# Attention score units: plain and diagonal ones merged three to two

## The chip, the cores and the metric

The program runs on one core of one Trainium2 chip. The metric is the device time of the whole program in microseconds, the median of several runs. Engines: TensorE (PE, its weight loads PEld), VectorE (DVE), ScalarE (ACT), GpSimd (POOL) and SyncE (SP), which issues the DMAs.

## What is computed

A transformer layer over 2048 tokens of width 512: layer norm, causal attention with 16 heads of 32, and beside it a feed-forward part with 4-bit weights. The change touches the attention alone. Cut to that:

```python
xn = _layernorm(x, axis=-1)
qkv = einsum('bsh,oh->bso', xn, w_qkv)            # 16 heads, head_dim 32
scores = einsum('bhqd,bhkd->bhqk', q, k) / sqrt(32)
scores = where(causal, scores, finfo.min)
probs = softmax(scores, axis=-1)
attn = einsum('bhqk,bhkd->bhqd', probs, v)
x = x + einsum('bsh,oh->bso', attn, w_o) + ffn(xn)
```

## The kernel before, in words

Three stages follow each other: layer norm and projection, attention (function `attention`), output projection and feed-forward. Attention takes the heads in eight pairs (`PAIRS`); `a` is the head of a pair, 0 or 1.

For each pair the scores are computed twice. The first time they stand plainly, queries on the partitions, only to find each query's largest score. A **unit** (`UNITS`, line 344; function `scores`, line 848, matmul at L855) is one such matmul: query tile `i` of 128 queries (16 of them) against up to 512 keys, key block `b`. For `b` under `i // 4` the unit lies left of the diagonal and is 512 columns wide. For `b == i // 4` it lies on the diagonal and is 128, 256, 384 or 512 wide (`P * (i % 4 + 1)`). A pair has 80 units: 48 left of the diagonal, 32 on it. They go round four banks (`p_s`). VectorE reduces each to its maximum (`unit_max`, line 759): L771 for the left ones, L767 with the mask for the diagonal ones. When the last unit of a query chunk `r` (four query tiles, `UNITS_TO[r]`) is reduced, VectorE joins the parts (`join_parts`, L778), GpSimd splits the maxima into three bf16 parts (`split`, five small instructions, L650 to L658), TensorE turns them (`turn_max`, L865, four small matmuls), and ScalarE copies them into rows of `q_stack` (`max_row`, L691), where the second computation of the scores subtracts them.

The second time the scores stand transposed, keys on the partitions. A pair has 40 steps (`STEPS`): chunk `qc` of 512 queries against key tile `kt`; each step has a **score tile** for each head (`scores_t`, L883; on the diagonal also `mask_t`, L892). The tiles go round three banks. ScalarE takes the exponential into `e_sb` (`exps`, L708), TensorE multiplies by the values (`product_v`, L909), GpSimd, at the end also VectorE, sums pairs of `e_sb` (`sum_steps`, L635 and L816) and TensorE sums those over the partitions (`row_sums`, L923). At a chunk's end ScalarE copies the output (`copy_out`, L720); GpSimd later multiplies it by the reciprocal sums (`normalise`, L668).

The order is written out. The loop `for k in range(NG)` (line 964) makes 80 **passes** of four steps each, ten to a pair; in this text pass 0 to 9 is `k` modulo 10. Pass `k` issues on TensorE: the eight score tiles of the *next* pass's steps, the first seven eighths of the pass's units in between, turned maxima if any are due, the row sums of the pass before, the products of this pass's steps, in passes 0, 2, 5, 9 (which multiply diagonal steps) also their row sums, and then the last eighth of the units. Score tiles on the diagonal (narrower, masked) are issued in passes 1, 4, 8 and 9: the **diagonal passes** of this text; the others are **plain passes**. In a plain pass two units follow the third tile, one the fourth, one the fifth, two the sixth, one the seventh. In a diagonal pass three follow the first two tiles, one the next two, two the next two, one the last two.

The units run ahead of the steps (`UNITS_AHEAD`, 56). The first pass takes 12 units, passes 1 to 72 take eight each, the last seven none. Units 1 to 44 stand earlier still, four or five behind each value tile of the stage's start. GpSimd's program in pass `k`: the second half of this pass's sums, the first half of the next's, the splits whose units end in this pass (`BATCHES[k]`), a `normalise` in passes 3, 4, 6, 7. The turns' passes (`TURNS`) don't depend on the units' order: chunk 0 in pass 8, chunk 1 in pass 9, chunk 2 in pass 1, chunk 3 in pass 4.

## Time and profile before

| | |
|---|---|
| median of 3 runs | 1840.53 us (1839.3 to 1840.86) |
| profiled execution | 1840.19 us, span 1838.4 us |
| TensorE busy | 1796.9 us, 98% |
| VectorE busy | 1127.0 us, 61% |
| ScalarE busy | 702.3 us, 38% |
| GpSimd busy | 721.6 us, 39% |
| plain score units L855 | 640 matmuls, 217.2 us busy |
| maxima L771 and L767 | 384 and 256 units, 241.2 and 119.7 us busy |
| sums on GpSimd L635 | 244, 291.2 us busy |

The span is the time from the first to the last instruction of the profiled execution; the run's time is 1.8 us longer. The first unit starts at 137 us, the passes run from 180 to 726 us, and the feed-forward part ends the span. Busy times are unions of recorded intervals. A matmul's record includes its way through the array, so TensorE counts as busy while it issues less than it could: what counts is the distance between starts.

### The profile page before, as it was taken

The numbers are of one execution on the slowest core, as the hardware profiler recorded it, in microseconds if no ns is written. First come the engines' busy times: TensorE is split into PE (matmuls) and PEld (weight loads), VectorE is DVE, ScalarE is ACT, GpSimd is POOL, SyncE is SP. The second block draws the span as 40 slices with busy tenths as digits, with TensorE's granted clock in tenths as the row PEclk, the third lists the DMA queues.
The fourth block names the chain that finished last, engine by engine and source line by source line (L and its number), as shares of the span: only waits on it lengthen the run. The fifth ranks groups of instructions, "written<-read, shape, count | busy, mean of one in ns | idle before, by whom it ended". The sixth has DMA issues, their size and how long they took to land.

```text
span 1838.4 us, 28874 instructions
## 1 busy us (share of the span) xinstructions
PE 1796.9 (98%) x10496; PEld 1348.4 (73%) x10496; DVE 1127.0 (61%) x1724; ACT 702.3 (38%) x1151; POOL 721.6 (39%) x720
## 2 busy tenths in 40 slices
PE   7989999999999998999999999999999999999998
PEld 6877666666666654478888888888888888888887
DVE  5416666666666666457665675666566567566654
ACT  3323666666666664023232332232232323323322
POOL 1431778778778774021222222222222222222221
PEclk9999999999999998999999999999999999999999
DMA  8675043143143100521101101100110110110002
GB/s 286 218 215 151 10 102 73 37 102 73 37 102 72 38 17 21 197 69 35 35 0 34 34 0 34 34 26 9 34 34 0 34 34 3 31 34 0 1 1 92
DMA packets 73105, 108.59 MB, mean 59 GB/s; under 512 B 24704, under 2 KB 44784, under 8 KB 69360
## 3 DMA queue, kind: packets, MB, share of 16 engines
q1 hardware_dynamic: 73008, 107.34, 21.2%
q8 instruction: 56, 0.92, 0.2%
q14 instruction: 41, 0.34, 0.1%
HBM read 74.04 MB, written 29.59 MB: 56 GB/s over the span
## 4 chain that ended last, share of the span: by engine, by line
PE 60%; DVE 0%; issue 0%
PE p_up L51 6%; PE p_gate L51 6%; PE p_gate L49 6%; PE p_up L49 6%; PE p_gate L50 6%; PE p_up L50 6%; PE p_out L51 6%; PE p_out L49 6%; PE p_out L50 6%; PE p_out L1358 1%; PE p_gate L1358 1%; PE p_up L1358 1%; DVE acc L1288 0%
## 5 line engine op out<-in xcount | busy, mean ns | idle before, releaser
L1200 POOL TENSOR_SCALAR poly<-poly 128x1024 f32<-128x1024 f32 (+1 forms) x65 | 71.4, 1098 | 841.3 <-ACT poly L1162 841.3
L635 POOL TENSOR_TENSOR e_sum<-e_sb 128x512 f32<-128x512 f32 (+1 forms) x244 | 291.2, 1220 | 99.2 <-PE p_o L923 89.8
L771 DVE TENSOR_REDUCE max_part<-p_s 128x1 f32<-128x512 f32 x384 | 241.2, 683 | 51.5 <-PE p_s L855 50.2
L708 ACT ACTIVATE e_sb<-p_v 128x512 f32<-128x512 f32 (+3 forms) x427 | 216.5, 552 | 129.7 <-PE p_v L883 70.2
L1263 DVE SCALAR_TENSOR_TENSOR inter<-inter,gate 128x1024 f32<-128x1024 f32 (+1 forms) x65 | 78.6, 1209 | 248.4 <-ACT inter L1168 247.6
L855 PE MATMUL p_s<-k_stack,q_stack 96*128 96x512 f32 (+3 forms) x640 | 217.2, 393 | 0.7 <-DVE max_part L771 0.5
L767 DVE CUSTOM_DVE_ANT_0 recip<-p_s,score_mask 128x128 bf16<-128x128 f32 (+3 forms) x256 | 119.7, 486 | 156.0 <-PE p_s L855 153.9
L1161 ACT ACTIVATE gate<-p_gate 128x1024 f32<-128x1024 f32 (+1 forms) x65 | 66.0, 1015 | 354.6 <-PE p_gate L51 354.6
L49 PE MATMUL p_gate<-xn_hi,w_hi 128*128 128x512 f32 x512 | 199.6, 390 | 0.0
L50 PE MATMUL p_gate<-xn_lo,w_hi 128*128 128x512 f32 x512 | 199.2, 389 | 0.0
L51 PE MATMUL p_gate<-xn_hi,w_lo 128*128 128x512 f32 x512 | 199.2, 389 | 0.0
L49 PE MATMUL p_up<-xn_hi,w_hi 128*128 128x512 f32 x512 | 199.2, 389 | 0.0
L50 PE MATMUL p_up<-xn_lo,w_hi 128*128 128x512 f32 x512 | 199.2, 389 | 0.0
L51 PE MATMUL p_up<-xn_hi,w_lo 128*128 128x512 f32 x512 | 199.2, 389 | 0.0
L49 PE MATMUL p_out<-i_hi,w_hi 128*128 128x512 f32 x504 | 196.1, 389 | 0.0
L50 PE MATMUL p_out<-i_lo,w_hi 128*128 128x512 f32 x504 | 196.1, 389 | 0.0
L51 PE MATMUL p_out<-i_hi,w_lo 128*128 128x512 f32 x504 | 196.1, 389 | 0.0
L1203 POOL TENSOR_TENSOR poly<-poly,gate 128x1024 f32<-128x1024 f32 (+1 forms) x65 | 177.8, 2735 | 5.4
L883 PE MATMUL p_v<-q_stack,k_stack 128*128 128x512 f32 (+3 forms) x427 | 159.2, 397 | 8.1 <-ACT e_sb L708 5.1
L855 PEld LDWEIGHTS p_s<-k_stack,q_stack 96*128 96x128 f32 x640 | 115.3, 189 | 47.0 <-issue 28.5
L909 PE MATMUL p_o<-e_sb,v_stack 128*32 128x256 f32 (+1 forms) x2304 | 148.6, 372 | 0.0
L1283 DVE TENSOR_TENSOR acc<-acc,p_out 128x2048 f32<-128x2048 f32 x63 | 143.6, 2280 | 3.3 <-PE p_out L51 3.3
(146 smaller groups left out, 3090.6 us busy)
## 6 DMA issues: line engine op xcount, KB each, us to landing
q_stack<-qk_scratch SPq DMA_DIRECT2D x48, 256.0 KB, 6.5
k_stack<-qk_scratch SPq DMA_DIRECT2D x48, 256.0 KB, 7.2
qk_scratch<-out_hi SPq DMA_DIRECT2D x32, 256.0 KB, 2.6
qk_scratch<-out_lo SPq DMA_DIRECT2D x32, 256.0 KB, 3.3
scales<-in_gate_up_s SPq DMA_DIRECT2D x128, 64.0 KB, 2.3
xn_lo_scratch<-xn_lo SPq DMA_DIRECT2D x4, 1024.0 KB, 5.2
v_scratch<-o_sb SPq DMA_DIRECT2D x16, 256.0 KB, 2.6
xn_lo<-xn_lo_scratch SPq DMA_DIRECT2D x1, 4096.0 KB, 16.7
```

The source lines that it names most:

```text
L49: nc.tensor.matmul(out, w_hi, x_hi, start=first, stop=False)
L50: nc.tensor.matmul(out, w_hi, x_lo, start=False, stop=False)
L51: return nc.tensor.matmul(out, w_lo, x_hi, start=False, stop=last)
L635: nc.gpsimd.tensor_tensor(*operands(k, i), ALU.add).then_inc(pool_summed, 1)
L708: nc.scalar.activation(e_sb[:, x % E_BUFS, 0:w], bank_st(x)[:, 0:w], ACT.Exp, scale=SCALE).then_inc(exp_done, 1)
L767: nc.vector.tensor_tensor_reduce(out=masked_scores[:, m % 2, 0:w], in0=p_s[:, slot[n] % S_BUFS, 0:w], in1=score_mask[:, W - w:], scale=1.0 ...
L771: nc.vector.reduce_max(part, p_s[:, slot[n] % S_BUFS, 0:w], AX.X).then_inc(maxed, 1)
L855: nc.tensor.matmul(p_s[:, slot[n] % S_BUFS, 0:w], q_stack[p % PB][a][0:ROWS, i * P:(i + 1) * P], k_stack[p % PB][a][0:ROWS, b * W:b * W + ...
L883: last = nc.tensor.matmul(bank_st(x)[:, 0:W - q0], k_stack[p % PB][a][:, kt * P:(kt + 1) * P], q_stack[p % PB][a][:, qc * W + q0:(qc + 1) ...
L909: last = nc.tensor.matmul(p_o[(2 * a + h) * D:(2 * a + h + 1) * D, 0, first - h * HALF:], v_stack[p % PB][:, kt, a, :], e_sb[:, (g * PIECE ...
L1203: nc.gpsimd.tensor_tensor(part_of(poly, h, parts), part_of(poly, h, parts), part_of(gate, h, parts), ALU.mult).then_inc(poly_done, 1)
L1283: nc.vector.tensor_tensor(here, here, p_out[:, :, :], ALU.add).then_inc(added, 1)
```

## The change

The list of units is put in another order. Before, it goes query tile by query tile: the left units of a tile, then its diagonal unit, for both heads. Now there are two lists, the left ones (`LEFT`) and the diagonal ones (`EDGE`), each in the order of query tiles, and five at a time are taken: one diagonal, two left, one diagonal, one left. Every unit keeps its operands and its width. `UNITS_TO` (after how many units a chunk's maxima are complete) was 8, 24, 48, 80 and is 19, 39, 59, 80. Head 1's first unit is the third instead of the second, hence `FIRST_OF`, where TensorE waits for the loaded heads.

```diff
-    UNITS = [(a, i, b, min(W, P * (i + 1) - b * W))
-             for r in range(TC) for i in range(4 * r, 4 * r + 4) for b in range(r + 1) for a in range(2)]
+
+    LEFT = [(a, i, b, W) for i in range(4, TT) for b in range(i // 4) for a in range(2)]
+    EDGE = [(a, i, i // 4, P * (i % 4 + 1)) for i in range(TT) for a in range(2)]
+    UNITS = [unit for n in range(TT) for unit in (EDGE[2 * n], LEFT[3 * n], LEFT[3 * n + 1], EDGE[2 * n + 1], LEFT[3 * n + 2])]
     NU = len(UNITS)
-    UNITS_TO = [sum(1 for a, i, b, w in UNITS if i < 4 * r + 4) for r in range(TC)]
+    UNITS_TO = [1 + max(u for u, (a, i, b, w) in enumerate(UNITS) if i < 4 * r + 4) for r in range(TC)]
     NUNIT = PAIRS * NU
+    FIRST_OF = [next(u for u, unit in enumerate(UNITS) if unit[0] == a) for a in range(2)]
...
-                if u < 2:
+                if u in FIRST_OF:
                     pe.wait_ge(qk_loaded[p % PB][a], 96 * (p // PB + 1))
```

The widths of a pass's eight units, worked out from the two lists (diagonal passes in bold):

| pass | before | now |
|---|---|---|
| 0 | 512 512 512 512 512 512 256 256 | 512 512 512 512 128 512 512 128 |
| **1** | 512 512 512 512 512 512 384 384 | 512 256 512 512 256 512 384 512 |
| 2 | 512 512 512 512 512 512 512 512 | 512 384 512 512 512 512 512 512 |
| 3 | 128 128 256 256 384 384 512 512 | 128 512 512 128 512 256 512 512 |
| **4** | 512 512 128 128 512 512 256 256 | 256 512 384 512 512 384 512 512 |
| 5 | 512 512 384 384 512 512 512 512 | 512 512 512 512 128 512 512 128 |
| 6 | 512 512 512 512 128 128 512 512 | 512 256 512 512 256 512 384 512 |
| 7 | 512 512 256 256 512 512 512 512 | 512 384 512 512 512 512 512 512 |
| **8** | 384 384 512 512 512 512 512 512 | 128 512 512 128 512 256 512 512 |
| **9** | 512 512 512 512 512 512 128 128 | 256 512 384 512 512 384 512 512 |

TensorE, pass 9 before, from the last score tiles to the first of the next pass (`p_s` are units, `p_v` and `p_st3` score tiles and their masks, `max_cols` the turned maxima, `p_o` row sums and products):

```order
L883 MATMUL p_v<-q_stack01,k_stack01 128x128
L892 MATMUL p_st3<-mask_k,ident_bf 128x128
L892 MATMUL p_v<-mask_k,ident_bf 128x128
L855 MATMUL p_s<-k_stack00,q_stack00 128x128
L865 MATMUL p_s<-ident_bf,max_cols 64x128 x4
L923 MATMUL p_o<-e_sum,ones 32x256 x8
...
L923 MATMUL p_o<-e_sum,ones 32x256 x2
L855 MATMUL p_s<-k_stack01,q_stack01 128x128
L883 MATMUL p_v<-q_stack00,k_stack00 128x512
```

The same place now:

```order
L886 MATMUL p_v<-q_stack01,k_stack01 128x128
L895 MATMUL p_st3<-mask_k,ident_bf 128x128
L895 MATMUL p_v<-mask_k,ident_bf 128x128
L858 MATMUL p_s<-k_stack00,q_stack00 128x512
L868 MATMUL p_s<-ident_bf,max_cols 64x128 x4
L926 MATMUL p_o<-e_sum,ones 32x256 x8
...
L926 MATMUL p_o<-e_sum,ones 32x256 x2
L858 MATMUL p_s<-k_stack00,q_stack00 128x512
L886 MATMUL p_v<-q_stack00,k_stack00 128x512
```

Units 7 and 8 of the pass were 128 wide and are 512 wide; nothing else moved.

TensorE, pass 1 before, from the first masks to the third and fourth score tile:

```order
L892 MATMUL p_v<-mask_k,ident_bf 128x128 x2
L855 MATMUL p_s<-k_stack00,q_stack00 128x512
L855 MATMUL p_s<-k_stack01,q_stack01 128x512
L855 MATMUL p_s<-k_stack00,q_stack00 128x512
L883 MATMUL p_st3<-q_stack00,k_stack00 128x384
```

The same place now:

```order
L895 MATMUL p_v<-mask_k,ident_bf 128x128 x2
L858 MATMUL p_s<-k_stack00,q_stack00 128x512
L858 MATMUL p_s<-k_stack00,q_stack00 128x256
L858 MATMUL p_s<-k_stack01,q_stack01 128x512
L886 MATMUL p_st3<-q_stack00,k_stack00 128x384
```

The second of the three units has 256 columns instead of 512.

GpSimd before, from the sums of pass 8 to those of pass 0 of the next pair (`max_cols` from `row_max` begins a split, `e_sum` are sums):

```order
L635 TENSOR_TENSOR e_sum<-e_sb_49 128x384 x2
L650 CAST max_cols<-row_max 128x2x4
L652 TENSOR_TENSOR rest1<-row_max,max_cols 128x2x4
L654 CAST max_cols<-rest1 128x2x4
L656 TENSOR_TENSOR rest2<-rest1,max_cols 128x2x4
L658 CAST max_cols<-rest2 128x2x4
L635 TENSOR_TENSOR e_sum<-e_sum,e_sb_49 128x256 x2
L635 TENSOR_TENSOR e_sum<-e_sum,e_sb_49 128x128 x2
L635 TENSOR_TENSOR e_sum<-e_sb_49 128x384 x2
L635 TENSOR_TENSOR e_sum<-e_sum,e_sb_49 128x256 x2
```

The same place now:

```order
L638 TENSOR_TENSOR e_sum<-e_sb_49 128x384 x2
L638 TENSOR_TENSOR e_sum<-e_sum,e_sb_49 128x256 x2
L638 TENSOR_TENSOR e_sum<-e_sum,e_sb_49 128x128 x2
L638 TENSOR_TENSOR e_sum<-e_sb_49 128x384 x2
L638 TENSOR_TENSOR e_sum<-e_sum,e_sb_49 128x256 x2
L638 TENSOR_TENSOR e_sum<-e_sum,e_sb_49 128x128 x2
L638 TENSOR_TENSOR e_sum<-e_sb_49 128x512 x2
L653 CAST max_cols<-row_max 128x2x4
L655 TENSOR_TENSOR rest1<-row_max,max_cols 128x2x4
```

The split of chunk 2 stood at the end of pass 8, ahead of the diagonal sums of pass 9. It now stands two passes later, at the end of pass 0, behind the diagonal sums of passes 9 and 0 and the first sums of pass 1.

## Rows read from the trace of the kernel before

**Rows 1.** One pair's length in windows: stretch, length, busy us per engine, granted clock, DMA.

```profile
199.00:268.00 69.00, 67.98 (x660) 42.93 (x658) 45.00 (x117) 42.97 (x92) 51.26 (x70) 1.00 0.31 66
```

**Rows 2.** ScalarE's timeline, pass 2: start, length, operation; the exponentials.

```profile
471.00 1.12 ACT L708 ACTIVATE e_sb<-p_v 128x512 f32<-128x512 f32 x2
471.95 0.66 ACT L708 ACTIVATE e_sb<-p_st 128x512 f32<-128x512 f32 x1
```

**Rows 3.** VectorE's timeline, pass 2 and the start of pass 3: maxima and a join.

```profile
469.77 3.68 DVE L771 TENSOR_REDUCE max_part<-p_s 128x1 f32<-128x512 f32 x6
...
476.60 0.19 DVE L778 TENSOR_REDUCE row_max<-max_part 128x8 f32<-128x32 f32 x1
```

**Rows 4.** Waits from 250 to 690 us: who for whom, us, times, longest.

```profile
PEld p_s L855 <- DVE max_part L771: 1.7, 7, 0.2
```

**Rows 5.** The same wait over the whole span.

```profile
PEld p_s L855 <- DVE max_part L771: 5.1, 15, 0.6
```

**Rows 6.** TensorE's weight loads, timeline in pass 5 of two pairs; idle before in brackets.

```profile
426.84 0.14 PEld L923 LDWEIGHTS p_o<-e_sb,ones 128*32 128x32 f32 x3 [0.77 <-POOL e_sum L635]
...
495.82 0.14 PEld L923 LDWEIGHTS p_o<-e_sb,ones 128*32 128x32 f32 x3 [0.77 <-POOL e_sum L635]
```

**Rows 7.** GpSimd's timeline, passes 4, 8 and 9; idle before in brackets.

```profile
487.42 4.46 POOL L635 TENSOR_TENSOR e_sum<-e_sb 128x512 f32<-128x512 f32 x4 [1.58 <-PE p_o L923]
...
515.35 4.46 POOL L635 TENSOR_TENSOR e_sum<-e_sb 128x512 f32<-128x512 f32 x4 [1.00 <-PE p_o L923]
519.74 0.23 POOL L650 CAST max_cols<-row_max 128x8 bf16<-128x8 f32 x1
...
521.03 2.25 POOL L635 TENSOR_TENSOR e_sum<-e_sum,e_sb 128x256 f32<-128x256 f32 x4
```

**Rows 8.** TensorE's timeline: unit 8 and the next tile (passes 9, 2), unit 7 (pass 0).

```profile
455.39 0.33 PE L855 MATMUL p_s<-k_stack,q_stack 96*128 96x128 f32 x1
455.55 0.45 PE L883 MATMUL p_v<-q_stack,k_stack 128*128 128x512 f32 x1
...
458.98 0.28 PE L855 MATMUL p_s<-k_stack,q_stack 96*128 96x256 f32 x1
459.13 0.50 PE L883 MATMUL p_st<-q_stack,k_stack 128*128 128x512 f32 x1
...
475.32 0.50 PE L855 MATMUL p_s<-k_stack,q_stack 96*128 96x512 f32 x1
475.66 0.40 PE L883 MATMUL p_v<-q_stack,k_stack 128*128 128x512 f32 x1
```

**Rows 9.** TensorE's timeline in diagonal passes: units 1 to 3 (pass 1), unit 7 (8, 9).

```profile
462.44 0.94 PE L855 MATMUL p_s<-k_stack,q_stack 96*128 96x512 f32 x3
463.22 0.34 PE L883 MATMUL p_st<-q_stack,k_stack 128*128 128x384 f32 x1
...
513.33 0.47 PE L855 MATMUL p_s<-k_stack,q_stack 96*128 96x512 f32 x1
513.74 0.35 PE L865 MATMUL p_s<-ident_bf,max_cols 128*64 128x128 bf16 x3
...
520.85 0.30 PE L855 MATMUL p_s<-k_stack,q_stack 96*128 96x128 f32 x1
521.08 0.41 PE L865 MATMUL p_s<-ident_bf,max_cols 128*64 128x128 bf16 x4
```

**Rows 10.** The first pass: VectorE's maxima, and TensorE's load for unit 10.

```profile
181.88 0.28 DVE L767 CUSTOM_DVE_ANT_0 recip<-p_s,score_mask 128x128 bf16<-128x128 f32 x1
...
182.29 3.67 DVE L771 TENSOR_REDUCE max_part<-p_s 128x1 f32<-128x512 f32 x6
...
183.63 0.19 PEld L855 LDWEIGHTS p_s<-k_stack,q_stack 96*128 96x128 f32 x1 [0.30 <-DVE max_part L771]
```

**Rows 11.** The longest pieces of the chain: start, us, what; the first matmuls behind attention.

```profile
731.16 9.96 PE p_gate L1358 x16
741.12 6.87 PE p_up L1358 x16
```

## The prediction, made before the kernel ran

> **What bounds the kernel now.** I read the page first, then attention in windows of one head pair, then one pair row by row, then the waits. TensorE was busy for 67.98 of the 69 us of a pair [rows 1], but that hides the real limit. Ten passes make one head pair, and they repeat: the same wait comes back at 426.84 and 495.82 [rows 6], 68.98 us apart. A pass has two halves. In the first, eight score tiles (L883) go round three banks: TensorE may write a tile only when ScalarE's exponential (L708) of the tile three back is done. The exponentials of wide tiles follow each other every 0.48 us (two from 471.00 on, the next at 471.95 [rows 2]), TensorE could deliver a wide matmul every 0.23 us (458.98 to 459.13 is 0.15 us with 256 columns; 475.32 to 475.66 is 0.34 us because a weight load isn't hidden [rows 8]). So in much of this half TensorE keeps step with ScalarE, and the plain score units (L855), which the change reorders, fill its gaps. In the second half TensorE alone sets the pace: row sums, products, and the eighth unit.
>
> Two engines that the change touches may give or take cover. VectorE takes the maxima, six wide ones in 3.68 us, 0.61 us each [rows 3]; it must stay within four banks of TensorE. It is busy 45.0 us in 69 [rows 1], and in 440 us of steady state TensorE's weight loads waited for it 1.7 us in all, never over 0.2 us [rows 4]. GpSimd is the fuller one, 51.3 us of 69 [rows 1], and TensorE waited for it once a pair, in pass 5: 0.77 us before the row sums at 495.82 [rows 6].
>
> **The change, part by part.** It removes and adds no matmul and no maximum. It moves three things.
>
> (a) *Widths inside a pass.* Units are numbered 1 to 8 as in the table above. What a narrow unit saves depends on who sets the pace where it stands.
>
> Unit 8 stands alone behind the products, on the path: to the start of the next score tile 0.34 us pass when it is 512 wide and 0.16 us when it is 128 (455.39 to 455.55) [rows 8]. A narrow one hides less of the weight load behind it, so I take 0.12 of these 0.18 us for a swap from 128 to 512, 0.07 from 384 to 512, nothing from 256 to 128. It gets wider in passes 1 (+0.07), 4 (+0.12) and 9 (+0.12), narrower in pass 5 (-0.12).
>
> Units 1 to 7 of a plain pass are paced by ScalarE where it is behind, as in passes 0, 3 and 6, in which it also copies the output. In pass 0 unit 7 grows from 256 to 512 columns: 0.15 us [rows 8] become 0.23, +0.08. In pass 6 it shrinks from 512 to 384, -0.07 at most by its columns, taken whole. In pass 7 units 3 and 4 grow from 256 to 512: 0.08 each, of which I take 0.14 in all. If this cover is complete both are 0.
>
> Units 1 to 3 of a diagonal pass (1, 4, 8, 9) stand between two pairs of tiles. In pass 1 three wide units take 0.78 us (462.44 to 463.22 [rows 9]) and TensorE sets the pace; pass 9 looks alike. They lose 256 and 384 columns, 0.12 and 0.17 us at 0.23 us for 512, but the second tile of the pair then waits for its exponential: -0.10 and -0.14. In passes 4 and 8 they hold 1152 before and after, and 1280 before and 1152 after: 0 and, as I read ScalarE's lead there, 0.
>
> Unit 7 of a diagonal pass stands before the turned maxima (L865) on the path: 0.23 us with 128 columns (520.85 to 521.08) against 0.41 us with 512 (513.33 to 513.74) [rows 9]. Pass 9 goes from the one to the other, +0.18; pass 4 from 256 to 512, between them, +0.12.
>
> By pass: 0: +0.08; 1: -0.03; 2, 3, 8: 0; 4: +0.24; 5: -0.12; 6: -0.07; 7: +0.14; 9: +0.16. Pass 4's unit 8 comes after the row sums on which GpSimd's chain for pass 5 starts, so its +0.12 only shortens the wait of 0.77 us. Sum: **+0.28 us a pair**. The ends, by columns: if all that units 7 and 8 gain is paid, 768 + 256 columns are +0.46 us; if all that units 1 to 3 of the diagonal passes lose counts and nothing added does, 768 columns are -0.35 us.
>
> (b) *VectorE's load.* Pass 2, with eight wide units, was its fullest (from 469.77 without a break [rows 3]); of the small waits in [rows 4] some 0.2 us a pair are its, and a 384-wide second unit takes them away: -0.07 a pair at the path, between 0 and -0.2. The joins of query chunks 0 to 2 now stand inside a pass: VectorE takes 0.19 us for one (476.60 [rows 3]), in engine time that it has.
>
> (c) *GpSimd's splits.* A split (L650 to L658) may run once its chunk's last unit is reduced. The chunks now end at units 19, 39, 59, 80 instead of 8, 24, 48, 80, so the splits of chunks 0, 1 and 2 move from passes 3, 5 and 8 to passes 5, 7 and 0 of the next pair. Each keeps GpSimd 1.3 us (519.74 to 521.03 [rows 7]). Leaving pass 3 gives nothing: GpSimd waited 1.58 us for TensorE behind it, at 487.42. In pass 5 one split replaces another, behind the sums that TensorE waits for. In pass 7 it eats the 1.00 us of idleness before 515.35 and delays the next sums by some 0.3 us; TensorE wants them a pass later, so 0. In pass 8 it goes away from ahead of pass 9's diagonal sums, which TensorE did not wait for: 0. In pass 0 it stands ahead of the turn of chunk 2 in pass 1, behind unit 7. Its unit is reduced some 8 us before that turn, and GpSimd has no more than its sums of the pass in between: 0, and without that cover up to its 1.3 us a pair.
>
> (d) *The start.* The first pass takes twelve units at once, and there VectorE sets the pace: unit 10 started at 183.63 when the maximum of unit 6 was done [rows 10]. Of the first six, two had 128 columns (0.41 us for both, 181.88 to 182.29). Now one of these is wide and the other 384: 0.61 + some 0.48, so +0.6 us once. Ahead of it, each burst of units behind a value tile now begins with a wide one, for whose maximum the fifth unit waits; it was narrow in five bursts. TensorE's loads waited 5.1 us for maxima in the whole trace [rows 5], 1.7 of them in steady state. Half a wait more for the five would be 1.4 us, none is 0; most of it hides behind matmuls under way, +0.2 us.
>
> **The sum.** Steady state +0.28 - 0.07 = +0.21 us a pair; 72 passes carry eight units, 7.2 pairs: +1.5 us. Start +0.8 us. Against the profiled execution's 1840.19 us (span 1838.4) that is 1842.5; that execution stands 0.3 us under the median, 1840.53, so the forecast of the median is **1842.8**. That is +0.12%, under the 0.2% (3.7 us) that a measurement of this kernel can tell from no change.
>
> A page speaks otherwise of VectorE. The row first: six wide maxima start and end within 3.68 us, so the next starts while the last still writes [rows 3]. The Trainium skill (VectorE: DVE Perf Modes, section The DRAIN you can't avoid) says that after each operation the pipe is emptied for about its duration less 266 ns before the next starts. By that, as an estimate from the page, a wide maximum would cost 0.6 us by duration and 0.35 us more, VectorE would be the bound of every pass, and since its total doesn't change, nor would a pair: the sum would be the start alone. The row contradicts it, and the sum goes by the row.
>
> **The rivals.**
> *Smoothing works (faster).* VectorE's and GpSimd's stalls shrink. For it: VectorE has 5.1 us of them [rows 5], GpSimd 0.77 us a pair [rows 6]. Against it: most of the first lie in the start, and GpSimd's chain from 487.42 to the sums at 495.82 (four sums, a product, four more) holds no split, so nothing leaves it. If all went: 1840.5 - 5.1 - 7 x 0.77 = 1830.0; half of it 1835. It decides where unit 5 to 7 of a wide pass now start earlier: 0.07.
> *Gains in the diagonal passes only.* -0.35 - 0.07 a pair and no losses: 1840.5 - 3.0 + 0.8 = 1838.3, within 0.2%: 0.12.
> *Wide units on the path (slower).* Units 7 and 8 are paid in full, 0.46 us, units 3 and 4 of passes 3, 5 and 7 lose their cover for another 0.3 us a pair, and the start costs its upper end, 2.0 us: 0.76 x 7.2 + 2.0 = +7.5, 1848.0. It decides where unit 7 is issued later than ScalarE frees its tile. For it: eight of ten seventh units are wide now, six before. Against it: ScalarE's copy of the output in passes 3 and 6. 0.22.
> *The split becomes the bound (slower).* (c) without cover, 1.3 us a pair: 1850. GpSimd would have to be several us later in pass 0: 0.03.
> *The clock at the hand-over.* TensorE's first 16 matmuls of the output projection took 9.96 us, the next 16 took 6.87 [rows 11]: it started at 1.2 GHz of its two levels. A shift of attention's end may add or take such a stretch, -3 to +3 us on top of any case, half the time nothing; it is in the range.
> That the order isn't what the change says has no chance left: TensorE's program shows the merge.
>
> **How the numbers follow.** The forecast case (1840 to 1844.2) has 0.56, the faster rival 0.07, the diagonal one 0.12, the slower ones 0.25. By sign, with some of the clock's swing: faster by over 0.2% (under 1836.9) 0.12, within 0.2% 0.62, slower (over 1844.2) 0.26. The range leaves out the far ends, 1835 and less and 1850, and reaches the slower rival's time: 1837.0 to 1848.0.
>
> **What would show it.** Right: pairs of 69.1 to 69.3 us; pass 5's wait for GpSimd still at 0.6 to 0.8 us; passes 4 and 9 longer by 0.1 to 0.25 us, pass 7 by 0.1; splits in passes 5, 7 and 0; unit 10 of the first pass 0.6 us later. Wrong: a pair under 68.7 us, pass 5's wait gone, or a wait of TensorE for GpSimd or for turned maxima that did not exist.

## The result, and the profile of the changed kernel

The changed kernel took 1846.16 us (median of 7 runs, 1843.42 to 1848.78) against 1840.76 us for the kernel before on the same chip: a ratio of 1.0027, 95% interval 1.0015 to 1.0039. Beside the last experiments it was measured again: 1844.79 us (11 runs) against 1840.66, 1.0024 with an interval of 1.0015 to 1.0033. By the medians it is 5.4 and 4.1 us slower, a little over the 0.2% that the forecast (+2.3 us, 1842.8) gave as the border, though both intervals begin below it. The profiled execution took 1843.77 us, its span 1842.0 us, 3.6 us more than before.

Where the 3.6 us are, from the starts of score tiles in both traces (L886 now, L883 before):

| place | before | now | longer by |
|---|---|---|---|
| first pass starts at | 179.21 | 180.47 | 1.26 |
| first pass | 7.52 | 8.24 | 0.72 |
| the other nine of the first ten | 61.93 | 62.45 | 0.52 |
| pairs 1 to 6, together | 413.78 | 414.91 | 1.13 |
| output projection starts at | 731.16 | 734.69 | 3.53 in all |

(The last pair's stretch is 0.1 us shorter now.) The start thus costs 1.98 us, the steady state 0.19 us a pair. The stretch behind attention is the same: the chain of the changed kernel (start, us, what), to be held against [rows 11]:

```profile
734.69 9.98 PE p_gate L1361 x16
744.67 6.87 PE p_up L1361 x16
```

One pair in windows (as [rows 1], the first window near the same place, the second from one pass 0 to the next). From one pass 0 to the next (455.55 to 524.53), TensorE was busy for 67.45 us before, VectorE for 45.01 and GpSimd for 55.63. TensorE's time has grown by 0.5 us, the others' have hardly moved, and no engine has become full:

```profile
200.00:269.00 69.00, 68.11 (x654) 42.16 (x650) 45.43 (x119) 42.98 (x92) 50.63 (x68) 1.00 0.29 63
458.65:527.75 69.10, 67.94 (x641) 41.98 (x640) 45.09 (x117) 42.98 (x92) 55.72 (x73) 1.00 0.33 71
```

TensorE's waits of the changed kernel from 250 to 690 us (who for whom, us in all, times, longest). VectorE's share is what it was [rows 4]; GpSimd's six waits, one a pair, fell from 0.77 to 0.55 us each:

```profile
PEld p_o L926 <- POOL e_sum L638: 3.3, 6, 0.6
...
PEld p_s L858 <- DVE max_part L770: 1.9, 6, 0.3
```

The wait itself, in pass 5, where [rows 6] had 0.77 us:

```profile
498.86 0.14 PEld L926 LDWEIGHTS p_o<-e_sb,ones 128*32 128x32 f32 x3 [0.54 <-POOL e_sum L638]
```

The ten passes of a pair, in us from one first score tile to the next, in each kernel that is told of below. The row of a kernel is that of its common pair: pairs 1 to 6 of one trace agree within 0.05 us in every pass, but for single long passes that are told of where they belong. Of *narrow at 3 or 5* it is the mean of its two variants:

| kernel | 0 | 1 | 2 | 3 | 4 | 5 | 6 | 7 | 8 | 9 | pair |
|---|---|---|---|---|---|---|---|---|---|---|---|
| before | 6.32 | 6.76 | 7.02 | 6.17 | 7.26 | 7.65 | 6.17 | 6.73 | 7.49 | 7.39 | 68.97 |
| changed | 6.22 | 6.84 | 6.95 | 6.16 | 7.49 | 7.36 | 6.22 | 6.73 | 7.48 | 7.71 | 69.15 |
| forecast, difference | +.08 | -.03 | -.07 | 0 | +.24 | -.24 | -.07 | +.14 | 0 | +.16 | +.21 |
| measured, difference | -.10 | +.08 | -.07 | -.01 | +.23 | -.29 | +.05 | 0 | -.01 | +.32 | +.19 |
| narrow last | 6.26 | 6.82 | 6.91 | 6.00 | 7.28 | 8.72 | 6.05 | 6.56 | 7.28 | 7.62 | 69.49 |
| wide last | 6.39 | 6.83 | 7.02 | 6.17 | 7.49 | 7.53 | 6.17 | 6.72 | 7.49 | 7.71 | 69.53 |
| split in pass 4 | 6.32 | 6.76 | 7.03 | 6.17 | 7.26 | 8.85 | 6.17 | 6.73 | 7.49 | 7.39 | 70.16 |
| narrow at 3 or 5 | 6.26 | 6.86 | 7.02 | 6.17 | 7.26 | 7.65 | 6.16 | 6.71 | 7.50 | 7.72 | 69.31 |
| placed | 6.20 | 6.66 | 6.82 | 6.04 | 7.31 | 7.48 | 6.04 | 6.49 | 7.27 | 7.42 | 67.73 |

(The forecast's pass 5 holds both its own -0.12 and the -0.12 by which pass 4's longer end was to shorten the wait.)

### The profile page after: what moved, and what is told of

It reads as the page before. It is cut to its first block, busy times and chain, and to the rows that moved or that the text cites. A ratio compares the mean times of both kernels' runs of the same rounds, so it can differ in the third digit from the quotient of the medians.

```text
span 1842.0 us, 28874 instructions
## 1 busy us (share of the span) xinstructions
PE 1801.9 (98%) x10496; PEld 1347.0 (73%) x10496; DVE 1128.0 (61%) x1724; ACT 702.7 (38%) x1151; POOL 723.3 (39%) x720
## 4 chain that ended last, share of the span: by engine, by line
PE 60%; DVE 0%; issue 0%
PE p_gate L51 6%; PE p_up L51 6%; PE p_gate L50 6%; PE p_gate L49 6%; PE p_up L50 6%; PE p_up L49 6%; PE p_out L51 6%; PE p_out L50 6%; PE p_out L49 6%; PE p_out L1361 1%; PE p_gate L1361 1%; PE p_up L1361 1%; DVE acc L1291 0%
## 5 line engine op out<-in xcount | busy, mean ns | idle before, releaser
L774 DVE TENSOR_REDUCE max_part<-p_s 128x1 f32<-128x512 f32 x384 | 256.7, 687 | 124.4 <-PE p_s L858 123.8
L770 DVE CUSTOM_DVE_ANT_0 recip<-p_s,score_mask 128x128 bf16<-128x128 f32 (+3 forms) x256 | 123.7, 483 | 85.8 <-PE p_s L858 83.7
L886 PE MATMUL p_v<-q_stack,k_stack 128*128 128x512 f32 (+3 forms) x427 | 160.2, 398 | 7.6 <-ACT e_sb L711 3.9
```

The lines of the kernel that those rows point to most:

```text
L770: nc.vector.tensor_tensor_reduce(out=masked_scores[:, m % 2, 0:w], in0=p_s[:, slot[n] % S_BUFS, 0:w], in1=score_mask[:, W - w:], scale=1.0 ...
L774: nc.vector.reduce_max(part, p_s[:, slot[n] % S_BUFS, 0:w], AX.X).then_inc(maxed, 1)
L886: last = nc.tensor.matmul(bank_st(x)[:, 0:W - q0], k_stack[p % PB][a][:, kt * P:(kt + 1) * P], q_stack[p % PB][a][:, qc * W + q0:(qc + 1) ...
```

## The experiments

All experiments but *the changed kernel again* hold one list of 80 units for each pair, `LISTS`: `OLD` is the order of before, `NEW` that of the change. What follows from a list (`UNITS_TO`, the splits' passes) is worked out from it as before.

### Which part of the time is the start's

The first kernel gives the first pair, whose units are those of the start, its old order and the others the new one, the second the other way round.

```diff
+    LISTS = [OLD] + [NEW] * (PAIRS - 1)
...
+    LISTS = [NEW] + [OLD] * (PAIRS - 1)
```

> The new order for head pairs 1 to 7, the old one for pair 0, so the start of attention is as it was before. Theory 'two parts' (the start costs 2.0 us once, each later pair 0.19 us): the first exponential starts at 176.2 us as before and not at 177.4, pairs take 69.16 us each, pass 9 is still 0.3 us longer, and the time is 1.3 to 1.7 us over the kernel before (ratio 1.0008). Theory 'steady state alone' (the start's delay is swallowed later): all of the 3.5 to 5 us stay, ratio 1.002 to 1.003.

> The other half: the new order for pair 0 alone, the old one for pairs 1 to 7. Theory 'two parts': first exponential at 177.4 us, unit 10 of the first pass some 0.7 us later still, pairs 1 to 6 at 68.97 us, time 2.0 to 2.3 us over before (ratio 1.0012). Theory 'steady state alone': within 0.5 us of before.

Medians: 1841.11 us for the first (ratio 1.0005, 0.9996 to 1.0014) and 1841.33 for the second (1.0009, 1.0000 to 1.0018): two halves that the time of the whole program can hardly tell from nothing. The traces can. Pairs take 69.15 us in the first and 68.94 in the second, the first pass 7.51 and 8.23. The stretch from the first unit to the first exponential, which holds the value tiles and their bursts, took 39.04 and 40.44 us, as in the kernels whose first pair they share (39.10 before, 40.46 changed). Its length has to be measured from its own first unit, since that starts anywhere from 137.0 to 140.7 us, whatever the kernel. In the seven traces here with the old first pair it took 38.99 to 39.10 us in five, and 39.31 and 39.40 in the two (*split in pass 4*, *narrow at 3 or 5*) in which TensorE's granted clock was still at 1.2 GHz when the first unit started; the three traces with the whole new first pair have 40.44 to 40.46. So the two costs belong to the two parts of the list and add up: +1.36 us ahead of the first pass, +0.72 in it, +0.19 a pair.

### The bursts behind the value tiles

```diff
+    def narrow_first():
+        out = list(NEW[:4])
+        for u in list(range(4, 44, 5)):
+            burst = NEW[u:u + 5]
+            out += sorted(burst, key=lambda unit: unit[3])
+        return out + NEW[44:]
+    LISTS = [narrow_first()] + [NEW] * (PAIRS - 1)
```

> The changed kernel, but in pair 0 each burst of units behind a value tile is sorted so that its narrowest unit comes first. Theory 'the fifth unit of a burst waits for the first one's maximum': the value stage takes 0.2 to 0.35 us less per burst, so the first exponential starts at 175.5 to 176.3 us instead of 177.4, and the time is 1.2 to 2 us under the changed kernel (ratio to before 1.0010 to 1.0016). Theory 'the sum of VectorE's work in the stage counts': first exponential stays at 177.4 us.

The median is 1842.78 us (1.0013, 1.0004 to 1.0023). The stretch took 38.62 us, 1.84 less than in the changed kernel and 0.48 less than before, with the same units in the same bursts. First pass and pairs are the changed kernel's (8.25, 69.15). TensorE's units in the changed kernel, in which every burst of five begins with a 512-wide unit and its last unit waits for the maximum of the first (in brackets the idle time and whom it waited for):

```profile
140.43 0.99 PE L858 MATMUL p_s<-k_stack,q_stack 96*128 96x512 f32 x4
...
141.61 0.39 PE L858 MATMUL p_s<-k_stack,q_stack 96*128 96x256 f32 x1 [0.19 <-DVE max_part L774]
...
144.58 1.62 PE L858 MATMUL p_s<-k_stack,q_stack 96*128 96x512 f32 x5
...
148.78 1.68 PE L858 MATMUL p_s<-k_stack,q_stack 96*128 96x512 f32 x5
```

The maximum that the fifth unit waited for, on VectorE:

```profile
140.87 0.69 DVE L774 TENSOR_REDUCE max_part<-p_s 128x1 f32<-128x512 f32 x1 [1.80 <-PE p_s L858]
```

Before, the third burst began narrow and was over sooner:

```profile
148.62 1.25 PE L855 MATMUL p_s<-k_stack,q_stack 96*128 96x256 f32 x5
...
152.46 1.50 PE L855 MATMUL p_s<-k_stack,q_stack 96*128 96x384 f32 x5
```

From burst to burst it is 4.15 to 4.26 us now, in all seven distances, and was 3.83 to 3.89 behind the three bursts that began with 128 or 256 columns before (148.62 to 152.46 is one). The brackets show 0.2 us of each wait. The rest hides in the pipelined records: the first four matmuls read 0.99 us, yet the fifth starts 1.18 us behind the first. In all traces it starts 1.18 us behind a first of 512 columns, 1.00 behind one of 384 and 0.81 or 0.82 behind one of 256.

Not all of the 1.36 us is this wait: 0.25 us lie between the first unit and the fifth of the stage (3.46 us now, 3.21 before), whose first four units hold 1280 columns instead of 768. The remaining 1.11 us are the bursts of five.

### Wide or narrow at the end of a pass

The first kernel sorts each pass's eight units by width, the second puts 128 columns at unit 8 and 256 at unit 7 wherever it has them; the first pair is the old one in both.

```diff
+    def wide_last():
+        out = []
+        for u in range(0, len(OLD), 8):
+            out += sorted(OLD[u:u + 8], key=lambda unit: unit[3])
+        return out
...
+    def narrow_last():
...
+            out.append(eighth.pop(0) if u % 8 == 7 else seventh.pop(0) if u % 8 == 6 and seventh else rest.pop(0))
```

> Pairs 1 to 7: the eight units of each pass of the old order, sorted so that the widest come last; no unit leaves its pass, chunk ends and splits stay. Pair 0 as before. Theory 'units 7 (diagonal passes) and 8 are on the path, others covered': pass 0 +0.1 us (unit 8 from 256 to 512), pass 1 +0.13, pass 4 +0.24 with pass 5 shorter by 0.1, pass 9 +0.3, the rest within 0.05, pairs at 69.5 to 69.7 us, ratio 1.0020 to 1.0030. Theory 'the mix of a pass decides' (VectorE's load per pass is unchanged): pairs at 68.97 us.

> Pair 0 as before; in pairs 1 to 7 the units are placed so that unit 8 of every pass is 128 wide (256 in passes 1 and 2) and unit 7 mostly 256. Theory 'place decides' (a narrow unit behind the products saves 0.12 us against a wide one, a narrow seventh 0.08 to 0.2 us in the passes where TensorE sets the pace there, elsewhere width is free): pass 2 to 8 each 0.1 to 0.2 us shorter, pairs at 67.9 to 68.4 us, time 4 to 7 us under before (ratio 0.997). Theory 'only the load on VectorE counts' (passes now hold up to seven wide units in a row): no gain, pairs at 68.9 to 69.5 us.

*Wide last* came to 1845.74 us (1.0022, 1.0013 to 1.0031), its pairs to 69.53 us, +0.56. It touches no chunk's order, so its splits stay, and the passes that got longer are those in which units 7 and 8 grew: 4 and 9 to exactly the changed kernel's 7.49 and 7.71. In pass 9 it gives units 1 and 2 only 128 columns, 768 fewer in all, and gets nothing for them: its pass 9 is as long as the changed kernel's.

*Narrow last* came to 1843.66 us (1.0020, 1.0011 to 1.0030), where 4 to 7 us less than before had been expected. Nine passes of its common pair sum to 60.77 us, against 61.32 before; pass 5 took 8.72 instead of 7.65 and ate twice that. The waits from 250 to 690 us name the place:

```profile
PEld p_o L941 <- POOL e_sum L653: 11.8, 6, 2.0
```

2.0 us a pair where there were 0.77. Its chunk 0 ended at unit 16, and so that split fell into pass 4, between the sums of pass 4 and those that pass 5's row sums wait for.

### The split, by itself

```diff
+    def swapped(u, v):
+        out = list(OLD)
...
+        out[u], out[v] = out[v], out[u]
+        return out
+    LISTS = [OLD] + [swapped(7, 8)] * (PAIRS - 1)
...
+    LISTS = [OLD] + [swapped(47, 56)] * (PAIRS - 1)
```

Both swap two units of 512 columns, so no width moves. In the first kernel, chunk 0 ends one unit later and its split goes from pass 3 to pass 4; in the second, chunk 2 ends nine units later and its split goes from pass 8 to pass 0.

> The old order with two units of the same width (512) exchanged in pairs 1 to 7, units 8 and 9 of the pair: chunk 0 ends one unit later, so its split moves from pass 3 to pass 4; widths, and all else, stay. Theory 'a split in pass 4 lies on the chain from the row sums of pass 3 to the diagonal sums of pass 5': pass 5 grows from 7.65 to 8.7 to 8.95 us, TensorE's wait for GpSimd in it from 0.77 to about 2.1 us, pairs at 70.0 to 70.3 us, 7 to 9 us in all, ratio 1.0040 to 1.0050. Rival 'GpSimd's order is free, it idles 1.6 us in pass 4': pairs at 68.97 us.

> The old order with two units of the same width (512) exchanged in pairs 1 to 7, so that chunk 2 ends at unit 57 instead of 48 and its split moves from pass 8 to pass 0 of the next pair, as in the changed kernel; widths stay. Theory 'covered': every pass within 0.02 us of before, pairs at 68.97 us, ratio 1.000. Rival 'the move out of pass 8 or into pass 0 is worth something': pass 9 shorter, or pass 0 or 1 longer, by 0.1 us or more.

The first came to 1850.22 us (1.0043, 1.0029 to 1.0056), the second to 1840.19 (0.9997, 0.9988 to 1.0006). One unit's place costs 1.2 us a pair, another's nothing. Pass 5 took 8.85 us (7.65 before), all other passes their old times. GpSimd of the first, from pass 4 on (start, us, line, operation, in brackets idle): the split's five instructions and the product between the sums of 493.09 and of 500.42, with no gap left:

```profile
493.09 4.46 POOL L649 TENSOR_TENSOR e_sum<-e_sb 128x512 f32<-128x512 f32 x4 [2.76 <-PE p_o L937]
497.49 0.23 POOL L664 CAST max_cols<-row_max 128x8 bf16<-128x8 f32 x1
...
498.65 0.22 POOL L672 CAST max_cols<-rest 128x8 bf16<-128x8 f32 x1
499.00 1.28 POOL L682 TENSOR_TENSOR acc<-acc,rsum_rows 64x512 f32<-64x512 f32 x1
500.42 2.23 POOL L649 TENSOR_TENSOR e_sum<-e_sum,e_sb 128x256 f32<-128x256 f32 x4
```

And TensorE's load of the row sums that ends the wait:

```profile
502.69 0.14 PEld L937 LDWEIGHTS p_o<-e_sb,ones 128*32 128x32 f32 x3 [1.95 <-POOL e_sum L649]
```

The long wait has a second price, paid now and then. In pair 6 of this kernel pass 6 took 7.11 us instead of 6.17, and in pairs 3 and 5 of *narrow last*, which waits as long, 7.10 instead of 6.05; no kernel with the short wait has such a pass 6. TensorE's granted clock was at the lower of its two levels there. Windows of *narrow last* behind its wait (stretch, length, busy us per engine, and, third from the end, the granted clock as a share of 2.4 GHz):

```profile
429.00:431.00 2.00, 0.54 (x8) 0.17 (x4) 0.00 (x0) 0.00 (x0) 2.00 (x4) 1.00 0.00 0
431.00:432.30 1.30, 1.06 (x14) 0.83 (x15) 0.11 (x1) 0.00 (x0) 1.30 (x2) 0.93 0.00 0
...
433.00:434.00 1.00, 1.00 (x4) 0.81 (x3) 0.09 (x1) 1.00 (x3) 1.00 (x2) 0.50 0.00 0
...
435.50:437.00 1.50, 1.50 (x8) 1.10 (x6) 1.50 (x3) 1.28 (x3) 1.50 (x2) 0.99 0.12 36
```

TensorE was busy for only 0.54 of the 2 us from 429 to 431, and from about 432.3 to 435.5 it was granted 1.2 GHz; that pass 6 took 1.05 us longer. In the other nine of the twelve pairs 1 to 6 of these two kernels the same wait was followed by no such stretch; which ones are hit, no run here tells.

The changed kernel escapes all this: its splits stand in passes 5, 7, 0 and, as before, 2, none in 4. The GpSimd rows of its pass 4 and 5 show the sums at 490.47, the product and the next sums, and the split only behind those:

```profile
490.47 4.45 POOL L638 TENSOR_TENSOR e_sum<-e_sb 128x512 f32<-128x512 f32 x4 [2.90 <-PE p_o L926]
495.15 1.29 POOL L671 TENSOR_TENSOR acc<-acc,rsum_rows 64x512 f32<-64x512 f32 x1 [0.23 <-POOL e_sum L638]
496.57 2.24 POOL L638 TENSOR_TENSOR e_sum<-e_sum,e_sb 128x256 f32<-128x256 f32 x4
498.76 2.53 POOL L638 TENSOR_TENSOR e_sum<-e_sb 128x512 f32<-128x512 f32 x2
501.23 0.23 POOL L653 CAST max_cols<-row_max 128x8 bf16<-128x8 f32 x1
```

The second experiment also holds a lesson on waits. TensorE waited 4.1 us for VectorE from 250 to 690 us, 14 times, where before it was 1.7 [rows 4], and its pairs took 68.95 us, no longer than before:

```profile
PEld p_s L869 <- DVE max_part L785: 4.1, 14, 0.3
```

### Can a narrow unit pay inside a diagonal pass?

Only passes 1 and 9 are touched (units 64 and 48 of a pair are their first).

```diff
+    def narrow_at(place):
...
+        out = list(OLD)
+        for first in (64, 48):
+            units = out[first:first + 8]
+            out[first:first + 8] = units[:place - 1] + units[6:] + units[place - 1:6]
+        return out
+    LISTS = [OLD] + [narrow_at(3 if p % 2 else 5) for p in range(1, PAIRS)]
```

> The order of before, but in passes 1 and 9 the two narrow units (384 and 128 columns) stand at units 3 and 4 (pairs 1, 3, 5, 7) or at units 5 and 6 (pairs 2, 4, 6) instead of 7 and 8, which are 512 wide. Theory: inside a diagonal pass ScalarE's exponentials set when the next tile or mask may be written, wherever the narrow unit stands, so it saves nothing, and units 7 and 8 cost their width: pass 9 7.70 us instead of 7.39 in all pairs, pass 1 6.83 to 6.88 instead of 6.76, a pair +0.4 us, the kernel +2.7 us. Rival (the prediction's step): the two passes' columns count at TensorE wherever they stand, less a small wait: pass 9 7.39 to 7.50, pass 1 6.76 to 6.80. Third: only units 5 and 6 pay, so the even pairs show 7.4 and the odd ones 7.7.

One execution, 1845.27 us, whose first unit also started late, at 140.68 us; what counts here are its passes. Pass 9 took 7.70 us with the narrow ones at 3 and 4 and 7.73 with them at 5 and 6, pass 1 6.85 and 6.87: no place among 3 to 6 pays for 768 or 256 columns. Pass 0 then gave 0.06 us back (6.26), so a pair is +0.34. TensorE in pass 9, units 3 and 4 at 128 columns; what is saved at 524.20 is waited for at 524.91, where ScalarE's exponential ends the wait:

```profile
524.20 0.30 PE L871 MATMUL p_s<-k_stack,q_stack 96*128 96x128 f32 x1
524.34 0.36 PE L899 MATMUL p_st<-q_stack,k_stack 128*128 128x256 f32 x1
524.91 0.38 PE L899 MATMUL p_v<-q_stack,k_stack 128*128 128x256 f32 x1 [0.21 <-ACT e_sb L724]
```

### Units placed by what they cost

The runs above say where a narrow unit pays: at unit 8 everywhere and at unit 7 of the diagonal passes. They also say where a chunk may not end: in the units of pass 4. A kernel with one plan for the first pair, narrow units at the front of its bursts, and another for the others puts this together. A plan gives each unit's width and, where it matters, its chunk; a row is one pass, from pass 3 on:

```diff
+    F, N, M, L = (W, None), (P, None), (2 * P, None), (3 * P, None)
+    STEADY = ([F] * 6 + [(2 * P, 0), (P, 0)]
+              + [F, (3 * P, 0), F, F, F, F, (2 * P, 0), (2 * P, 1)]
+              + [F] * 6 + [(3 * P, 0), (P, 0)]
+              + [F] * 6 + [(3 * P, 1), (P, 1)]
...
+    LISTS = [fill(START)] + [fill(STEADY)] * (PAIRS - 1)
```

> An order made for the places: unit 8 of every pass and unit 7 of the diagonal passes narrow (128 or 256), splits in passes 5, 7, 0 and 2 (never in pass 4), in pair 0 each burst behind a value tile begins narrow and the first pass begins with four narrow units. Theory 'places and the split in pass 4': passes 2, 3, 5, 6, 7 each 0.12 to 0.17 us shorter than before, pass 8 0.3 us, pass 9 unchanged; pairs at 67.6 to 68.0 us; first exponential 0.4 to 0.8 us sooner after the first unit (38.3 to 38.7 us), first pass 0.4 us shorter; in all 8 to 10 us under before, ratio 0.9945 to 0.9955. Theory 'narrow-last orders lose' (the 0.5 us a pair that the run with narrow units last lost come from its seven wide units in a row): pairs over 69 us, ratio over 1.001.

It took 1831.75 us (1829.27 to 1833.15, 5 runs), a ratio of 0.9950 with an interval of 0.9937 to 0.9964: faster than both kernels, and as expected. The stretch from the first unit to the first exponential took 37.89 us, the first pass 7.07, and most pairs 67.73. Pairs 1 and 6 lost 1.2 and 1.1 us, however, in pass 2 alone (8.05 and 7.92 us instead of 6.82). There VectorE was to take the reciprocals of the row sums (L829, `invert_sums`), for which the DMA that loads them (`sums_loaded`) had not landed, and the maxima queued behind:

```profile
261.87 0.35 DVE L829 RECIPROCAL rcompact<-compact 128x32 f32<-128x32 f32 x1 [1.49 <-DMA compact<-sum_scratch]
...
262.14 3.01 DVE L816 TENSOR_REDUCE max_part<-p_s 128x1 f32<-128x512 f32 x5
```

TensorE waited for VectorE right after:

```profile
262.82 0.19 PEld L900 LDWEIGHTS p_s<-k_stack,q_stack 96*128 96x128 f32 x1 [0.83 <-DVE max_part L816]
```

In the kernel before, with longer passes, that reciprocal never waited. The last experiment moves it:

```diff
-                if p and s == 8:
-                    invert_sums(p - 1)
                 units = units_of(k)
...
                 for n in units:
                     unit_max(n)
+                    if p and s == 8 and n == units[3]:
+                        invert_sums(p - 1)
```

> The kernel whose units are placed by hand, a second time, beside the next one. 1830 to 1833 us. Pass 2 takes 6.82 us in most pairs and about 8 us in those where the load of the row sums is late; if that is a matter of the DMA's moment, other pairs or another number of them are hit than pairs 1 and 6.

> As the placed kernel, but VectorE takes the reciprocals of the row sums behind the fourth unit of pass 2 instead of ahead of the first. Theory: the two long passes 2 (8.05 and 7.92 us) come from VectorE's wait for the load of the row sums (1.49 and 1.36 us), behind which the maxima queue; 2 us later the load has landed, every pass 2 takes 6.82 us, the span is 2.3 us shorter than the placed kernel's in its first profile (some 1827.6) and the median 1 to 2 us lower. Rival: the reciprocals then reach GpSimd too late for pass 3's product, GpSimd falls behind and pass 5 gets longer than 7.48 us. Second rival: something else stops TensorE there and the long passes stay.

The placed kernel, run again, had its long pass 2 in pair 6 alone (7.91 us, 6.90 in pair 2), and took 1830.24 us (0.9940, 0.9926 to 0.9953). With the reciprocals later every pass 2 took 6.82 us, the reciprocals never waited, pass 5 stayed at 7.48, and the span was 1826.6 us, 1.8 under the other's. The rows of pair 6 of both, VectorE, first the placed one:

```profile
600.12 0.35 DVE L829 RECIPROCAL rcompact<-compact 128x32 f32<-128x32 f32 x1 [1.36 <-DMA compact<-sum_scratch]
600.39 3.01 DVE L816 TENSOR_REDUCE max_part<-p_s 128x1 f32<-128x512 f32 x5
```

```profile
599.65 2.48 DVE L816 TENSOR_REDUCE max_part<-p_s 128x1 f32<-128x512 f32 x4 [0.48 <-PE p_s L902]
602.05 0.34 DVE L829 RECIPROCAL rcompact<-compact 128x32 f32<-128x32 f32 x1
```

The mechanism is shown, a gain in time is not: the median was 1831.12 us (0.9945, 0.9932 to 0.9959), and the two intervals overlap almost wholly.

### The changed kernel again

> The changed kernel once more, beside the placed ones, for its ratio to before and for a second profile. If the start's cost belongs to the order and not to one execution: the first exponential 40.4 to 40.5 us behind the first unit and a first pass of 8.24 us again, pairs of 69.15 us, and a ratio of 1.002 to 1.003.

Its trace repeats the first to 0.02 us: 40.46 us from the first unit to the first exponential, a first pass of 8.25, pairs of 69.15. The start's cost belongs to the order and not to one execution.

## Why the forecast came out as it did

The direction was right and the steady state close, +0.19 us a pair against +0.21. The median lies 3.4 us over the forecast, in the range, and just past the border that I had given 0.26. The profiled execution, 1843.77 us, lies 1.3 us over its own forecast of 1842.5, and the start below is 1.3 of that. The other 2.1 us are that the median of these runs stands 2.4 us over their profiled execution (0.2 us when measured again), which no run here explains.

**(d), the start: this is the term that was mis-sized.** The first pass was right (+0.6 forecast, +0.72). The bursts were forecast at +0.2 us, between 0 and 1.4; the stretch that holds them got 1.36 longer, 0.25 of that ahead of the first burst of five, where the forecast had put nothing. The step that failed is "most of it hides behind matmuls under way". I had the mechanism, the fifth unit behind the maximum of the burst's first, and took its price from the idle times in brackets, which show only a part of it. The distance between the bursts' starts shows all of it, and it stood in the trace of before: 3.84 us from 148.62 to 152.46, behind a burst that begins narrow, and 4.26 from 144.36 to 148.62, behind a wide one. Both the old first pair (1.42 us back) and narrow units at the front of the same bursts (1.84 us back) confirm it. With 1.36 in place of 0.2 the sum would have been 1844.0.

**(a), units 7 and 8: right.** Pass 4 +0.23 (forecast +0.24). Pass 5 -0.29 (-0.24): the load that ends the wait stands 6.60 us into the pass (492.26 to 498.86) instead of 6.73 (489.09 to 495.82), which is the 0.12 forecast, and the narrow unit 8 gives the other 0.17. The bracket shrank by more, 0.23 us, because TensorE also reached the load 0.1 us later. *Wide last* and *narrow at 3 or 5* pay the same prices at the same places. The 0.12 for unit 8 instead of its bare 0.18 holds as well: the pass behind it gave 0.06 back. Its second tile starts 0.23 us behind its first where unit 8 was wide and 0.28 where it was narrow (pass 0 now and before). The rest of pass 0's -0.10 stands at its own unit 8, from 256 to 128 columns, which I had put at nothing: 0.16 us to the next tile instead of 0.22.

**(a), units 1 to 3 of a diagonal pass: wrong.** -0.10 and -0.14 for passes 1 and 9 did not come. I had read from [rows 9] that three wide units make TensorE set the pace, and overlooked that the second tile of the pair behind them waits for ScalarE in any case. In pass 9 its weight load starts 1.39 us into the pass before (517.15 to 518.54) and 1.39 now (520.04 to 521.43), and the masks behind it 1.70 us (518.85) and 1.68:

```profile
520.04 0.40 PE L886 MATMUL p_v<-q_stack,k_stack 128*128 128x512 f32 x1
...
521.43 0.19 PEld L886 LDWEIGHTS p_v<-q_stack,k_stack 128*128 128x128 f32 x1 [0.20 <-ACT e_sb L711]
521.72 0.28 PE L895 MATMUL p_v<-mask_k,ident_bf 128*128 128x128 bf16 x2
```

*Narrow at 3 or 5* extends that to units 3 to 6.

**(a), plain passes: where ScalarE sets the pace, the cover was complete.** The +0.08 of pass 0's seventh unit, the +0.14 of pass 7 and the -0.07 of pass 6 were all nil or of the other sign. Pass 0's eighth tile starts 3.58 us into the pass with a 256-wide seventh unit (455.55 to 459.13 [rows 8]), 3.60 with a 512-wide one:

```profile
462.02 0.39 PE L858 MATMUL p_s<-k_stack,q_stack 96*128 96x512 f32 x1
462.25 0.42 PE L886 MATMUL p_st<-q_stack,k_stack 128*128 128x512 f32 x1
```

So the sum of (a) came out right by luck: gains and losses that were both not there, -0.24 and +0.15, nearly cancelled. Pass 6's +0.05 is the give-back of unit 8 the other way: the pass now stands behind a narrow unit 8 instead of a wide one. Its second tile starts 0.29 us behind its first instead of 0.24 and its first product 4.02 us into the pass instead of 3.97, as in *narrow last* (0.29, 4.02), whose pass 5 ends narrow too.

**(b)** Pass 2 got 0.07 us shorter, as forecast. It isn't the wide unit 8 ahead of it in pass 1: *wide last* and *narrow at 3 or 5* have that too, with a pass 2 of 7.02 us. That VectorE's waits are why is argued, not shown, and the second experiment on the split warns: more of them cost nothing elsewhere.

**(c)** Right for this change: no split cost anything. The split as the bound has its mechanism, though, in another pass than I named. In pass 0 it is free, in pass 4 it costs 1.2 us a pair (*split in pass 4*), within 0.1 of the 1.3 that the rival put on it. The rule that the change obeyed by chance is that no chunk may end in the units of pass 4.

**The page on VectorE.** By the rule of the Trainium skill (VectorE: DVE Perf Modes, section The DRAIN you can't avoid) as the prediction told it, VectorE would have been the bound and a pair the same as before. A pair moved by 0.19 us, and at TensorE's places, units 7 and 8, so the row decided rightly. The prediction left out a sentence of the same paragraph, "A next op that is not held starts earlier"; the six maxima in 3.68 us [rows 3] agree with that.

**The rivals.** *Wide units on the path* had its sign and its place at units 7 and 8, but units 3 and 4 kept their cover. Its price for the start, 2.0 us, is what the start cost, 1.98. Nothing bore out *smoothing works* or *gains in the diagonal passes only*. *The clock* did the same at the hand-over in both kernels: the first 16 matmuls took 9.96 and 9.98 us.

Left open: why runs of one program spread so far, the changed kernel's from 1843.1 to 1848.8 us and before's from 1837.8 to 1843.3. The traces say where it could come from. From the first unit to the last pair the two of the changed kernel agree within 0.02 us (529.11 and 529.09), and from the first matmul of `p_up` to the end all fourteen take 1097.4 to 1097.5 us. What differs whatever the order is when the first unit starts (3.7 us), the last pair's pass 4 (1.6 us, below) and the hand-over, from the first matmul of `p_gate` to the first of `p_up` (8.6 us with the first pair's old order, 9.5 to 10.0 elsewhere). No trace of one of the long runs exists to confirm it.

## What to carry to other kernels

Independent filler work on a bound engine isn't smoothed by averaging its sizes: a small piece is worth its size only where nothing else sets the next start, so find these places from distances between starts and put the small pieces there. Here that, together with narrow units at the front of the first pair's bursts, took 0.5% off with the same instructions. What an order drags along (a chain on another engine that starts when a group is complete) can cost more than the order gains, and is tested by a swap that changes nothing else. When passes get shorter, look for the loads that used to land just in time.

## What the runs showed that I had not expected

- A wait for VectorE that grew from 1.7 to 4.1 us in 440 us had no effect on the pairs (68.97 and 68.95 us), while an idle time of 0.2 us in brackets stood for some 0.3 to 0.4 us between bursts. Neither is a price.
- The load of the row sums, issued alike in every pair, let VectorE wait 1.49 and 1.36 us in two of seven pairs, and in a second execution of the same program 1.36 in one and 0.35 in another.
- A clock that falls or not behind the same idle time. In the last pair, whose passes hold no units from pass 3 on, pass 4 took 8.5 to 8.7 us in some executions (before and the changed kernel among them) and 6.97 in others, whatever the kernel. The windows of before, from 692 us, show 0.64 and 0.51 of 2.4 GHz behind two stretches in which TensorE was busy for 1.6 of 2 us:

```profile
688.00:690.00 2.00, 1.60 (x15) 0.70 (x6) 0.00 (x0) 0.79 (x2) 1.49 (x2) 1.00 0.00 0
690.00:692.00 2.00, 1.55 (x9) 0.94 (x9) 0.00 (x0) 1.71 (x5) 0.00 (x0) 1.00 0.00 0
692.00:694.00 2.00, 2.00 (x23) 1.10 (x27) 0.00 (x0) 1.73 (x5) 0.00 (x0) 0.64 0.00 0
694.00:696.00 2.00, 2.00 (x24) 0.91 (x20) 1.29 (x2) 0.01 (x1) 1.22 (x1) 0.51 0.00 0
```

  The kernel with the first pair's old order, 3.7 us later in its span, has the same two gaps and no such fall:

```profile
692.00:694.00 2.00, 1.60 (x12) 0.86 (x8) 0.00 (x0) 1.09 (x2) 1.27 (x1) 1.00 0.00 0
694.00:696.00 2.00, 1.56 (x11) 1.02 (x10) 0.00 (x0) 1.54 (x5) 0.00 (x0) 1.00 0.00 0
696.00:698.00 2.00, 2.00 (x37) 1.25 (x40) 0.51 (x1) 1.61 (x4) 0.45 (x1) 1.00 0.00 0
```

- The first unit started anywhere from 136.97 to 140.68 us in the span, whatever the kernel. Together with the 1.6 us of the last pair's pass 4 that is more than the change itself, and it is the reason why stretches are measured from their own beginnings here.
